# Group-norm chains, row norm, key landmarks and half the bias product rearranged in a two-stage attention kernel

## Chip, cores and metric

The kernel runs on one core of one Trainium2 chip. The metric is the device time of one execution in microseconds. TensorE does the matrix products, VectorE the reductions and elementwise work, ScalarE the activations and copies, GpSimd some elementwise work and the indirect DMAs, and SyncE issues most other DMAs. Each engine runs its own queue in order; semaphores join them.

## What is computed

16 images of 128 channels and 32x32 pixels (N = 1024) pass through six blocks, each added to its input: attention over pixels behind a group norm, convolutions behind a second group norm, landmark attention behind a row norm, a mixture of 8 experts with 2 chosen a row, a plain attention, and a mixture of 16 experts with 6 chosen. What the change touches, cut down:

```python
# block 1 and 2: norm over 8 groups (with weight and bias), then over 32 groups
xn = (xg - mean) * rsqrt(var + 1e-5);  xn = xn * norm_w + norm_b
# block 3: landmark attention, 8 heads of 16, 16 landmarks (every 64th row)
q, k, v = layernorm(t) @ Wqkv.T + bqkv
q_lm, k_lm = q[::64], k[::64]
kernel_1 = softmax(q @ k_lm.T * scale)
kernel_2 = softmax(q_lm @ k_lm.T * scale)
kernel_3 = softmax(q_lm @ k.T * scale)
z = kernel_2.T / sum(kernel_2 ** 2)
for _ in range(6): z = 2 * z - z @ kernel_2 @ z
t = t + (kernel_1 @ (z @ (kernel_3 @ v))) @ Wproj.T + bproj
# block 4: each row goes to its 2 best of 8 experts
scores = top2(softmax(layernorm(t) @ Wg))
t = t + sum_e scores[:, e] * (gelu(x @ W1[e] + b1[e]) @ W2[e] + b2[e])
```

## The kernel before

The program has four stages. **The first stage** (`attention_phase`) is the attention over pixels. Image by image, 64 slots (8 heads by 8 row tiles) go by; each holds a scores product that is read by a maximum on VectorE (L454), and a product with the shift (L693), an exponential on ScalarE (L597) and a product with the values (L706). Beside these, `plan` puts the next image's group norm into the first slots (`normed`: moments, the groups' sums, norm, the query, key and value products) and the previous image's projection and second group norm into slots 29 to 34 (`projected`). A ring of two PSUM banks (`ps_a`) is shared by the scores and these products: TensorE (PE) may write a bank only when VectorE or ScalarE has read what lay in it two uses before.

The group norm: the channels' moments (`channel_moments`, L75 to L80), a small product for the groups' sums (L655), then `group_affine` (L85 to L95): mean and mean of squares, variance, `rsqrt` by an integer guess and three Newton steps (L58 to L67), scale and shift. Each small VectorE operation is followed by a drain, so they make a chain. "norm" (L491 to L496) folds weight and bias in and writes the input `xn` of the query product (L663); "norm2" (L480 to L482) stores scale and shift in `gn2` for later and writes the normed second input, which "turn2" (L485) transposes.

**The convolutions** (`conv_phase`) follow and are untouched.

**The second stage** (`landmark_and_gelu_phase`) does the landmark attention and the 8 experts. `experts(i)` goes through 46 slots; in the even ones TensorE multiplies a 128-row tile by its expert's first weights (L1793), in the odd ones the tile before by the second weights (L1803), and ScalarE takes the gelu between them (L1609). Beside them run `front(i + 2)` (the landmark attention of the image two ahead), `choice(i + 1)` (row norm, router and row numbers of the next image) and `combine(i - 1)` (gathered results added, L1532). These are generators: `yield 17` means that what follows is placed behind the experts' own work of slot 17, in the queue of that engine. In one slot the order is experts, front, choice, combine. Ahead of the loop `front(0)` runs alone and `front(1)` beside `choice(0)`.

What the steps touch, by engine:

- Row norm of `choice`: `token_norm_steps` yields after each half of the statistics (n = 0, 1), after the variance (n = 2), after `rsqrt` (n = 3) and twice in the writes of the normed rows (L983). L1493 (`if n == 2: yield 4`) leaves the statistics and the variance in slot 0 and puts `rsqrt` and the writes in slot 4. TensorE turns the rows in slots 8 and 9 (L1738).
- In slot 4, ahead of that, `front` multiplies the convolutions' result in (L1336, L1338), behind the gate product (L1654, slot 2); TensorE turns the result in slot 6 (L1664).
- Landmarks: the query product (slot 15) and key product (slot 16) go to PSUM (L1654); ScalarE adds the biases (`qt` L1568, `kt` L1571); VectorE spreads the landmark columns over the heads (L1346, twice) in slot 17; TensorE multiplies all queries by the key landmarks in slot 18 (L1677) and all keys by the query landmarks in slot 19.
- Newton steps: slots 25 to 36, one product each that VectorE copies (L1398), and two that it takes from 2z (L1401, L1402). Beside the first step it sums `kernel_1`'s weights (L1406, L1408), beside the second it multiplies by the inverse (L1411). `k1_exp` says that ScalarE's exponentials of these weights are through.
- Bias product: scores times the experts' second bias, in two halves through one PSUM bank `pc` (L1768, slots 34 and 36); VectorE adds each half to the rows (L1518, slots 36 and 38) and then lets the bank go (`base_up`).
- Row numbers: VectorE's routing (L1441 on, slots 27 on) ends in `index_out` (L1465). GpSimd then scatters the normed rows to DRAM in expert order (L1313, 16 indirect DMAs), SyncE loads the first four tiles (L1238), TensorE turns them in the last slot (L1776) and ScalarE copies them (L1623).

**The dense stage** (`dense_attention_and_silu`) shares `token_norm_steps` and with it `rsqrt`.

## Time and profile before

| | us |
|---|---|
| median of 3 runs (5480.68 to 5505.98) | 5484.53 |
| the profiled execution | 5477.94 |
| its span, first to last instruction | 5476.1 |
| PE busy | 4820.5 (88%) |
| DVE busy | 3578.8 (65%) |
| ACT busy | 2948.8 (54%) |
| POOL busy | 1017.9 (19%) |
| mean granted clock of TensorE | 0.953 |

The engines are named PE (TensorE, matmul), PEld (its weight loads), DVE (VectorE), ACT (ScalarE), POOL (GpSimd) and SP (SyncE); a q behind a name means the engine's queue, as in SPq. All rows come from the profiled execution; times count from the start of its span. Busy time is no measure of the bound where stages differ, so the rows below go by stage. In a timeline the number in brackets is how long the engine stood idle before the instruction, and behind the arrow is what ended that. A granted clock of 1.00 is TensorE's upper level (2.4 GHz), 0.50 the lower (1.2 GHz).

### The profile page before, as it was taken

To read this page: it belongs to the slowest core of one execution; us is meant where nothing else is said; L and a number is where in the kernel's file an instruction comes from. 1 tells how busy PE (TensorE), PEld (TensorE's weight loads), DVE (VectorE), ACT (ScalarE), POOL (GpSimd) and SP (SyncE) were. 2 spreads that over 40 slices of the span, in tenths; PEclk is the share of its full clock that TensorE was granted. 3 is DMA by queue.
4 is the path that set the end of the run, shared out by engine and by line. 5 is a ranking of instruction groups with operands and counts; after the bars stand their busy time and mean duration, and the time that the engine had idled before them with its cause. 6 is when DMAs were issued, how large, how long until landed. Compare 5 with 4: busy or idle time off the path is not lost.

```text
span 5476.1 us, 81744 instructions
## 1 busy us (share of the span) xinstructions
PE 4820.5 (88%) x25601; PEld 2609.5 (48%) x25601; DVE 3578.8 (65%) x7699; ACT 2948.8 (54%) x5390; POOL 1017.9 (19%) x1348
## 2 busy tenths in 40 slices
PE   5888888888888886967999899999899999999999
PEld 1222222222222221335888888888755555555554
DVE  6677777777776772646666666665676766766765
ACT  2555566555655654423555555556655455555552
POOL 2211211121212212211434334343200000000000
PEclk7999999999999998987999999999999999999999
DMA  2522222222222221222555455554311111111112
GB/s 85 147 71 71 76 89 71 71 71 71 71 83 71 72 74 32 30 68 83 154 165 173 140 176 154 164 170 116 109 49 46 52 46 48 51 43 52 51 46 74
DMA packets 406296, 477.08 MB, mean 87 GB/s; under 512 B 87640, under 2 KB 249648, under 8 KB 403760
## 3 DMA queue, kind: packets, MB, share of 16 engines
q1 hardware_dynamic: 372128, 424.84, 25.5%
q0 software_dynamic: 20576, 35.55, 2.4%
q10 hardware_dynamic: 13168, 11.48, 0.8%
q8 instruction: 213, 3.49, 0.3%
q14 instruction: 211, 1.73, 0.1%
HBM read 308.54 MB, written 145.57 MB: 83 GB/s over the span
## 4 chain that ended last, share of the span: by engine, by line
PE 30%; DVE 12%; issue 4%; ACT 4%; DVEq 3%; POOL 2%; DMA 1%; ACTq 0%; SPq 0%; POOLq 0%
PE n_ps_f L2155 4%; PE n_ps_f L2148 4%; PE n_ps_xy L1803 3%; PE n_ps_h L1793 3%; PE n_ps_c L2195 2%; PE n_ps_h L2207 2%; POOL rows_scratch L1313 2%; PE n_ps_f L2142 2%; PE n_ps_f L1654 1%; PE n_ps_xy L2211 1%; PE n_ps_h L2211 1%; DVEq L2027 1%; DVE n_down_weights L2026 1%; PE n_ps_f L995 1%; ACT n_hidden L1609 1%
## 5 line engine op out<-in xcount | busy, mean ns | idle before, releaser
L597 ACT ACTIVATE a_probs<-ps_b 128x512 f32<-128x512 f32 x2048 | 1110.7, 594 | 800.4 <-PE ps_b L693 787.5
L454 DVE TENSOR_REDUCE a_negmax<-ps_a 128x1 f32<-128x1024 f32 x1024 | 1206.4, 1219 | 384.5 <-PE ps_a L637 374.8
L637 PE MATMUL ps_a<-a_k_stack,a_q_stack 96*128 96x512 bf16 x2048 | 635.6, 397 | 181.4 <-DVE a_negmax L454 89.8
L693 PE MATMUL ps_b<-a_q_stack,a_k_stack 99*128 99x512 bf16 x2048 | 675.0, 392 | 67.5 <-ACT a_probs L597 30.6
L1609 ACT ACTIVATE n_hidden<-n_ps_h,n_b 128x128 f32<-128x128 f32 x1472 | 420.4, 374 | 402.6 <-PE n_ps_h L1793 399.1
L706 PE MATMUL ps_o<-a_probs,a_v_ones 128*32 128x512 f32 x4096 | 561.8, 621 | 0.2 <-ACT a_probs L597 0.2
L637 PEld LDWEIGHTS ps_a<-a_k_stack,a_q_stack 96*128 96x128 bf16 x2048 | 146.3, 99 | 736.4 <-DVE a_negmax L454 470.2
L1803 PE MATMUL n_ps_xy<-n_down_weights,n_hidden 128*128 x2944 | 402.6, 280 | 56.1 <-ACT n_hidden L1609 30.2
L693 PEld LDWEIGHTS ps_b<-a_q_stack,a_k_stack 99*128 99x128 bf16 x2048 | 196.7, 100 | 486.4 <-ACT a_probs L597 247.0
L1803 PEld LDWEIGHTS n_ps_xy<-n_down_weights,n_hidden 128*128 128x128 f32 x2944 | 363.4, 193 | 86.7 <-issue 83.1
L2092 ACT ACTIVATE n_down_weights<-n_ps_h 128x512 f32<-128x512 f32 x288 | 172.4, 599 | 427.7 <-PE n_ps_h L2207 318.5
L1793 PE MATMUL n_ps_h<-n_xy,n_up_weights 128*128 128x128 f32 x2944 | 397.8, 279 | 3.1 <-DMA n_up_weights<-in_L_ffn_W_dram 1.7
L1313 POOL DMA_INDIRECT rows_scratch<-n_xln,n_index_out x256 | 256.9, 1004 | 719.2 <-DVE n_index_out L1465 642.3
L1793 PEld LDWEIGHTS n_ps_h<-n_xy,n_up_weights 128*128 128x128 f32 x2944 | 366.7, 194 | 26.1 <-issue 23.2
L1305 POOL DMA_INDIRECT n_rows<-outs_scratch,n_index_back x256 | 259.0, 1012 | 357.3 <-DMA outs_scratch<-n_xy 254.3
L410 POOL CAST a_shift<-a_shift 16x128 bf16<-16x128 f32 x192 | 54.0, 281 | 1315.1 <-DVEq L463 1297.7
L2155 PEld LDWEIGHTS n_ps_f<-n_xln,n_u_probs_t 128*128 128x128 f32 x2048 | 246.4, 192 | 59.8 <-issue 44.2
L2155 PE MATMUL n_ps_f<-n_xln,n_u_probs_t 128*128 128x128 f32 x2048 | 251.2, 276 | 1.6 <-ACT n_u_probs_t L2058 1.6
L2148 PE MATMUL n_ps_f<-n_qt 128*128 128x512 f32 x512 | 240.9, 593 | 0.0
L1977 DVE TENSOR_REDUCE e_negmax<-n_ps_f 128x1 f32<-128x1024 f32 x128 | 156.6, 1224 | 116.6 <-PE n_ps_f L2148 116.6
L2061 ACT ACTIVATE n_yt_probs<-n_ps_f,e_negmax 128x1024 f32<-128x1024 f32 x128 | 142.6, 1114 | 118.9 <-DVE e_negmax L1977 118.5
L2195 PE MATMUL n_ps_c<-n_down_weights,n_xt 128*128 128x512 f32 x384 | 198.8, 601 | 4.4 <-DVE n_down_weights L2033 4.4
(350 smaller groups left out, 7485.5 us busy)
## 6 DMA issues: line engine op xcount, KB each, us to landing
n_up_weights<-in_L_ffn_W_dram SPq DMA_DIRECT2D x368, 256.0 KB
n_up_weights<-score_scratch SPq DMA_DIRECT2D x512, 128.0 KB, 2.9
split_scratch<-a_pieces SPq DMA_DIRECT2D x180, 256.0 KB
a_q_stack<-split_scratch SPq DMA_DIRECT2D x128, 192.0 KB, 3.4
a_k_stack<-split_scratch SPq DMA_DIRECT2D x128, 192.0 KB, 4.0
rows_scratch<-n_zero SPq DMA_DIRECT2D x16, 1472.0 KB
outs_scratch<-n_xy SPq DMA_DIRECT2D x176, 128.0 KB
n_xg<-rows_scratch SPq DMA_DIRECT2D x80, 256.0 KB, 4.7
```

Source lines behind the costliest of these rows:

```text
L454: dve.tensor_reduce(negmax[:, b, t:t + 1], bank, axis=AX.X, op=ALU.max, negate=True).then_inc(ring_read, 1)
L597: act.activation(probs[:, m % PROBS, 512 * k:512 * k + 512], ps_b[:, k, :], ACT.Exp).then_inc(b_exp, 1)
L637: last = pe.matmul(bank[:, cols], q_stack[0:KS, h, 128 * t:128 * t + 128], k_stack[0:KS, h, cols], start=True, stop=True)
L693: pe.matmul(ps_b[:, k, :], k_stack[:, h, 128 * t:128 * t + 128], q_stack[:, h, 512 * k:512 * k + 512], start=True, stop=True).then_inc(b_u ...
L706: last = pe.matmul(ps_o[32 * j:32 * j + 32, 512 * k:512 * k + 512], v_ones[:, t, J * g + j, :], probs[:, (J * quad + j) % PROBS, 512 * k:5 ...
L1313: gp.indirect_dma_start(x_dram[i][:, :], bass.IndirectOffsetOnAxis(index_out[:, k, t:t + 1], 0), xln2[:, t, :], None).then_inc(scattered, 16)
L1609: last = act.activation(hidden[:, j % 2, f, :], ps_h[j % 2][:, 128 * f:128 * f + 128], ACT.Gelu, bias=b1[:, bass.ds(e, 1), f:f + 1].rearra ...
L1793: last = pe.matmul(ps_h[j % 2][:, 128 * f:128 * f + 128], up_weights[:, j % RING, 128 * f:128 * f + 128], rows_t, start=True, stop=True)
L1803: last = pe.matmul(ps_xy[:, col:col + 128], hidden[:, j % 2, f, :], own_down[:, f, :], start=(f == 0), stop=(f == FT - 1))
L2148: last = pe.matmul(pa[:, 512 * k:512 * k + 512], qt[:, 128 * t:128 * t + 128], qt[:, 512 * k:512 * k + 512], start=True, stop=True)
L2155: last = pe.matmul(pb[:, 0:C], probs_t[:, (t - 1) % 2, m, :], xln[:, m, :], start=(m == 0), stop=(m == NT - 1))
L2195: last = pe.matmul(ps_o[:, :], wd(unit), mixed[(i * STEPS + n) % 3], start=False, stop=(unit == UNITS - 1), skip_group_check=True)
```

## The change

`rsqrt` no longer makes a negative half of its input first: the factor goes into an operation that was there, so it has 10 operations for 11. A new `rsqrt_column` for one column takes minus half of the variance and needs 7. `group_affine` becomes `group_scale`: it forms minus half of the variance directly and leaves the shift to its callers. "norm" needs one operation for the shift where it had two, and "norm2" writes the scale straight into `gn2` and makes the shift there. In the second stage, the key landmarks are made from the key product in PSUM, with the bias added in the same operation; ScalarE's copy of the keys waits for them, and the product of all keys waits for that copy. The sum of `kernel_1`'s weights moves ahead of the first Newton step, its inverse stays where it was. The row norm's `rsqrt` goes to slot 0. The second half of the bias product goes from slot 36 to 39, VectorE's part of it from 38 to 40.

```diff
 def rsqrt(dve, y, v, t):
     dve.tensor_scalar(y.bitcast(I32), v.bitcast(I32), -0.5, 1597463007.0, ALU.mult, ALU.add)
-    dve.drain()
-    dve.tensor_scalar(v, v, -0.5, None, ALU.mult)
     for _ in range(3):
         dve.drain()
         dve.tensor_tensor(t, y, y, ALU.mult)
         dve.drain()
-        dve.tensor_tensor(t, t, v, ALU.mult)
+        dve.scalar_tensor_tensor(t, t, -0.5, v, ALU.mult, ALU.mult)
         dve.drain()
         last = dve.scalar_tensor_tensor(y, t, 1.5, y, ALU.add, ALU.mult)
...
+def rsqrt_column(dve, out, y, minus_half, t):
+
+    dve.tensor_scalar(y.bitcast(I32), minus_half.bitcast(I32), -0.5, 519526879.0, ALU.mult, ALU.add)
+    dve.drain()
+    for n in range(3):
+        dve.scalar_tensor_tensor(t, y, minus_half, y, ALU.mult, ALU.mult)
+        dve.drain()
+        dve.scalar_tensor_tensor(out if n == 2 else y, t, 1.5, y, ALU.add, ALU.mult)
+        dve.drain()
...
-def group_affine(dve, scale, shift, group, sums, sums_read, width, small, eps):
+def group_scale(dve, scale, group, sums, sums_read, width, small, eps):
     dve.tensor_scalar(group[:, :], sums, 1.0 / width, None, ALU.mult).then_inc(sums_read, 1)
     dve.drain()
-    dve.tensor_tensor(small[:, 0:1], group[:, 0:1], group[:, 0:1], ALU.mult)
+    dve.scalar_tensor_tensor(small[:, 0:1], group[:, 0:1], 0.5, group[:, 0:1], ALU.mult, ALU.mult)
     dve.drain()
-    dve.tensor_tensor(small[:, 1:2], group[:, 1:2], small[:, 0:1], ALU.subtract)
+    dve.scalar_tensor_tensor(small[:, 1:2], group[:, 1:2], -0.5, small[:, 0:1], ALU.mult, ALU.add)
     dve.drain()
-    dve.tensor_scalar(small[:, 1:2], small[:, 1:2], 0.0, eps, ALU.max, ALU.add)
+    dve.tensor_scalar(small[:, 1:2], small[:, 1:2], 0.0, -0.5 * eps, ALU.min, ALU.add)
     dve.drain()
-    rsqrt(dve, scale, small[:, 1:2], small[:, 2:3])
-    dve.scalar_tensor_tensor(shift, group[:, 0:1], -1.0, scale, ALU.mult, ALU.mult)
-    dve.drain()
+    rsqrt_column(dve, scale, small[:, 0:1], small[:, 1:2], small[:, 2:3])
...
                 elif what == "norm2":
-                    dve.tensor_copy(gn2[:, 0, bass.ds(prev, 1)], gscale[:, :])
-                    dve.tensor_copy(gn2[:, 1, bass.ds(prev, 1)], gshift[:, :])
-                    dve.tensor_scalar(xn[:, :], x1[:, :], gscale[:, :], gshift[:, :], ALU.mult, ALU.add)
+                    scale, shift = gn2[:, 0, prev:prev + 1], gn2[:, 1, prev:prev + 1]
+                    dve.scalar_tensor_tensor(shift, group[:, 0:1], -1.0, scale, ALU.mult, ALU.mult)
+                    dve.drain()
+                    dve.tensor_scalar(xn[:, :], x1[:, :], scale, shift, ALU.mult, ALU.add)
...
                     dve.tensor_tensor(gscale[:, :], gscale[:, :], nw[:, :], ALU.mult)
-                    dve.tensor_tensor(gshift[:, :], gshift[:, :], nw[:, :], ALU.mult)
                     dve.drain()
-                    dve.tensor_tensor(gshift[:, :], gshift[:, :], nb[:, :], ALU.add)
+                    dve.scalar_tensor_tensor(gshift[:, :], group[:, 0:1], gscale[:, :], nb[:, :], ALU.mult, ALU.subtract)
                     dve.drain()
-                    dve.tensor_scalar(xn[:, :], xf[:, :], gscale[:, :], gshift[:, :], ALU.mult, ALU.add).then_inc(xn_up, 1)
+                    dve.tensor_scalar(xn[:, :], xf[:, :], gscale[:, :], gshift[:, :], ALU.mult, ALU.subtract).then_inc(xn_up, 1)
...
-                for src, dst, up in ((qt, q_lm, 1), (kt, k_lm, 2)):
-                    dve.wait_ge(S["qk_up"], i * 2 + up)
-                    last = dve.tensor_tensor(dst[:, :].rearrange("p (h l) -> p h l", h=HEADS), b16,
-                                             src[:, 0:N:STEP].unsqueeze(1).broadcast_to((128, HEADS, LM)), ALU.mult)
-                last.then_inc(S["lm_up"], 1)
+                every = lambda ap: ap[:, 0:N:STEP].unsqueeze(1).broadcast_to((128, HEADS, LM))
+                by_head = lambda ap: ap[:, :].rearrange("p (h l) -> p h l", h=HEADS)
+                dve.wait_ge(S["qk_up"], i * 2 + 1)
+                dve.tensor_tensor(by_head(q_lm), b16, every(qt), ALU.mult)
+                dve.wait_ge(S["qk_ps"], i * 2 + 2)
+                dve.scalar_tensor_tensor(by_head(k_lm), every(pa), kb[:, :], b16, ALU.add, ALU.mult).then_inc(S["lm_up"], 1)
...
                 dve.tensor_scalar(zt[:, :], m2[:, :], fro[:, :], None, ALU.mult).then_inc(S["z0_up"], 1)
+                dve.wait_ge(S["k1_exp"], i + 1)
+                dve.tensor_reduce(sum1[:, :], k1v, axis=AX.X, op=ALU.add)
+                dve.drain()
...
                     if it == 0:
-                        dve.wait_ge(S["k1_exp"], i + 1)
-                        dve.tensor_reduce(sum1[:, :], k1v, axis=AX.X, op=ALU.add)
-                        dve.drain()
                         dve.reciprocal(sum1[:, :], sum1[:, :])
...
-                    if n == 2:
+                    if n == 3:
                         yield 4
...
-                    yield 36 + 2 * k
+                    yield 36 + 4 * k
                     dve.wait_ge(S["b2_ps"], i * HALVES + k + 1)
...
                 act.wait_ge(S["qk_ps"], i * 2 + 2)
+                act.wait_ge(S["lm_up"], i + 1)
                 act.activation(kt[:, :], pa[:, :], ACT.Identity, bias=kb[:, :]).then_inc(S["qk_up"], 1)
...
                 yield 19
+                pe.wait_ge(S["qk_up"], i * 2 + 2)
                 wide(pa, q_lm[:, :], kt).then_inc(S["s3_ps"], 1)
...
-                    yield 34 + 2 * k
+                    yield 34 + 5 * k
                     if k:
                         pe.wait_ge(S["base_up"], i * HALVES + 1)
```

## Rows read from the trace of the kernel before

**Rows 1.** Busy time by stretch: start:end, us, busy of each engine (instructions), PEclk, DMA, GB/s.
```profile
92.00:2082.00 1990.00, 1745.94 (x8524) 489.80 (x8524) 1416.24 (x1835) 1184.66 (x2105) 404.38 (x673) 0.96 0.25 79
2472.00:3840.00 1368.00, 1219.34 (x9231) 1100.34 (x9232) 836.05 (x2911) 757.85 (x1896) 476.56 (x480) 0.96 0.50 150
```

**Rows 2.** Waits of PE, 2472 to 3840 us: total us, times, longest.
```profile
PE n_ps_c L1738 <- DVE n_xln L983: 22.7, 16, 3.2
PE n_ps_c L1768 <- DVE maps L1518: 20.5, 16, 1.4
PE n_ps_xy L1803 <- ACT n_xy L1623: 17.8, 17, 1.3
PE n_ps_f L1702 <- DVE n_small L1398: 15.8, 32, 1.2
PE n_ps_f L1677 <- DVE n_small L1346: 11.3, 15, 1.6
```

**Rows 3.** PE in order of time, one image: start, us, line, tiles, xcount [idle before].
```profile
2989.35 1.04 PE L1664 MATMUL n_ps_f<-c_ident,n_u_probs_t 128*128 128x128 f32 x8
...
3035.42 0.49 PE L1702 MATMUL n_ps_f<-n_small 128*128 128x128 f32 x2 [0.67 <-DVE n_small L1398]
...
3063.89 0.44 PE L1776 MATMUL n_ps_xy<-c_ident,n_xg 128*128 128x128 f32 x2 [0.95 <-DMA n_xg<-rows_scratch]
```

**Rows 4.** DVE in order of time, the same image.
```profile
2985.76 1.28 DVE L1336 SCALAR_TENSOR_TENSOR n_u_probs_t<-n_ps_f,n_b,n_u_probs_t 128x1024 f32<-128x1024 f32 x1 [3.24 <-PE n_ps_f L1654]
...
2996.23 0.17 DVE L58 TENSOR_SCALAR n_inv<-n_var 128x8 int32<-128x8 int32 x1
...
2999.01 2.14 DVE L983 TENSOR_SCALAR n_xln<-n_tok_next,n_mv,n_inv 128x128 f32<-128x128 f32 x8
...
3010.73 0.38 DVE L1346 TENSOR_TENSOR n_small<-c_block,n_kt 128x128 f32<-128x128 f32 x1 [2.89 <-ACT n_kt L1571]
...
3026.72 0.29 DVE L1398 COPY n_small<-n_ps_f 128x128 f32<-128x128 f32 x1 [1.59 <-PE n_ps_f L1699]
...
3028.64 1.22 DVE L1406 TENSOR_REDUCE n_sum<-n_xln 128x64 f32<-128x1024 f32 x1
...
3037.05 0.17 DVE L1465 CAST n_index_out<-n_place 128x16 uint32<-128x16 f32 x1
```

**Rows 5.** Line L1336, all of it: idle time before, ended by: us, times.
```profile
  PE n_ps_f L1654: 27.0, 16
```

**Rows 6.** ACT in order of time, the same image.
```profile
3009.57 1.13 ACT L1571 ACTIVATE n_kt<-n_ps_f,n_kb 128x1024 f32<-128x1024 f32 x1
```

**Rows 7.** Busy time by stretch, 7 us behind the bias product, two images of 14.
```profile
3049.00:3056.00 7.00, 7.00 (x64) 6.88 (x63) 3.71 (x12) 1.77 (x6) 5.17 (x7) 1.00 0.31 101
3135.00:3142.00 7.00, 7.00 (x49) 6.88 (x48) 2.15 (x8) 0.85 (x2) 5.17 (x7) 0.76 0.33 111
```

**Rows 8.** POOL in order of time, first and last of 16 scatters.
```profile
3038.00 0.99 POOL L1313 DMA_INDIRECT rows_scratch<-n_xln,n_index_out  x1 [31.30 <-DVE n_index_out L1465]
...
3057.46 1.27 POOL L1313 DMA_INDIRECT rows_scratch<-n_xln,n_index_out  x1 [0.30 <-issue]
```

**Rows 9.** SP in order of time: the load of the scattered rows.
```profile
3060.99 0.38 SPq L1238 DMA_DIRECT2D n_xg<-rows_scratch  x1
```

**Rows 10.** DVE in order of time, first stage, two images.
```profile
1067.92 3.58 DVE L454 TENSOR_REDUCE a_negmax<-ps_a 128x1 f32<-128x1024 f32 x3 [2.05 <-PE ps_a L637]
...
1256.02 0.81 DVE L496 TENSOR_SCALAR a_xn<-a_xf,a_gscale,a_gshift 128x1024 f32<-128x1024 f32 x1
1256.96 2.36 DVE L454 TENSOR_REDUCE a_negmax<-ps_a 128x1 f32<-128x1024 f32 x2
```

**Rows 11.** Waits of PE, 92 to 2082 us.
```profile
PE ps_a L663 <- DVE a_negmax L454: 13.0, 12, 1.6
```

**Rows 12.** PE in order of time, first stage, one image.
```profile
1255.24 1.18 PE L637 MATMUL ps_a<-a_k_stack,a_q_stack 96*128 96x512 bf16 x4 [1.73 <-DMA a_k_stack<-split_scratch]
...
1258.24 3.78 PE L663 MATMUL ps_a<-a_xn,a_wqkv 128*128 128x512 f32 x4 [0.96 <-DVE a_negmax L454]
```

More of the change, by code:

```diff
@@ L477, in step @@
                     width, eps = ((C // 8, 1e-5), (C // 32, 1e-5))[work[1]]
-                    group_affine(dve, gscale[:, :], gshift[:, :], group, bank[:, 0:2], ring_read, width, small, eps)
+                    scale = gn2[:, 0, prev:prev + 1] if work[1] else gscale[:, :]
+                    group_scale(dve, scale, group, bank[:, 0:2], ring_read, width, small, eps)
                 elif what == "norm2":
-                    dve.tensor_copy(gn2[:, 0, bass.ds(prev, 1)], gscale[:, :])
-                    dve.tensor_copy(gn2[:, 1, bass.ds(prev, 1)], gshift[:, :])
-                    dve.tensor_scalar(xn[:, :], x1[:, :], gscale[:, :], gshift[:, :], ALU.mult, ALU.add)
+                    scale, shift = gn2[:, 0, prev:prev + 1], gn2[:, 1, prev:prev + 1]
+                    dve.scalar_tensor_tensor(shift, group[:, 0:1], -1.0, scale, ALU.mult, ALU.mult)
+                    dve.drain()
+                    dve.tensor_scalar(xn[:, :], x1[:, :], scale, shift, ALU.mult, ALU.add)
                     dve.drain()
```

## The prediction

> **What bounds the kernel now.** I read the views in this order: the busy time by stage, TensorE's waits inside the second stage, one image of that stage on each engine in order of time, and the same for one image of the first stage. The attention over pixels (first stage) takes the span's first 2.19 ms, the convolutions go on to 2.39 ms, the landmark attention with the experts (the second stage, to which five of the six edits belong) lasts until about 3.84 ms, and the dense attention takes the rest. In both stages that the change touches TensorE is the engine nearest to full: 88% of the first loop, 89% of the second; VectorE has 71% and 61% [rows 1]. Both stages are one order written by hand, so each engine is an in-order queue, and time is lost where TensorE stands at a wait. So a cut on VectorE is worth only what it takes from a wait of TensorE, and a wait removed is worth only what the next wait doesn't take back.
>
> In the second stage the waits repeat from image to image, with a period of 85.5 us: on average 1.4 us for the turn of the row norm's result (22.7 over 16), 1.3 for the second half of the bias product (20.5 over 16), 0.75 for the product with the key landmarks (11.3 over 15), and in the Newton steps two that make 0.25 and 0.67 in each of the loop's 14 images (with those ahead of the loop 15.8 over 32) [rows 2, 3]. These the change is aimed at. Two others matter for where the gain goes: the rows for the next image's experts come by DMA at the end of each image (0.95 of wait in the image shown), and behind them TensorE waits 1.05 for ScalarE's copy (17.8 over 17) [rows 2, 3].
>
> **The change, part by part.** I price against the profiled execution, 5477.94 us with a span of 5476.1; the median of the three runs, 5484.53, lies 6.6 us above it, and I take that distance over to the changed kernel.
>
> *Row norm.* The inverse root of the experts' row norm (11 small VectorE operations; 2.78 us, by the same sequence of the other norm [rows 4]; 10 now, some 2.53) moves from behind the u product (slot 4) to ahead of it (slot 0). Its result was 1.4 us late for TensorE; 2.78 us earlier it isn't late any more. What it moves ahead of is the product L1336, for which VectorE sits idle until TensorE's L1654 is through: 27.0 us over 16, on average 1.7, in the loop mostly 0.7 to 3.2 [rows 4, 5]. The root takes more than that in most images, so L1336 starts up to 1.8 us later. TensorE needs the result at L1664: from the start of L1336 (2985.76) it and L1338 take 2.59 us, to 2988.35, and L1664 starts at 2989.35 [rows 3, 4]. So 0.9 us of the delay are free, and up to 0.9 could show as a new wait. I take nothing for it, since the wait for rows at the end of the image gives VectorE a longer idle time there (below). Of the 22.7 us I take 20: in the image ahead of the loop nothing lies beside the chain, and most of the wait remains.
>
> *Key landmarks.* VectorE read the key landmarks from ScalarE's biased copy and waited 2.89 us for it [rows 4]; now it reads the product itself, complete some 2.2 us earlier. TensorE's wait is gone, 11.3 us, and about 1 more in the first image, ahead of that stretch. The new operation (PSUM operand, a bias column, 128x128) isn't in the trace; a copy of this size from PSUM takes 0.29, the operation replaced 0.38 [rows 4]; I take 0.38, and the difference hides in those 2.2 us at either end. The added wait stands in ScalarE's queue: its copy of the keys now follows VectorE's landmarks, and behind it are a copy of rows and an expert's activations. ScalarE began that copy at 3009.57, after other work [rows 6]; the landmarks would be ready near 3008.9, so the wait is met. The product with all keys, which gets a wait of its own, stands behind two more groups of TensorE's queue, some 3 us after the copy's end: nothing.
>
> On this the Trainium skill's PSUM — Partial Sum Buffer, section "PSUM bank collisions raise a hardware error", says that two engines mustn't read one bank at once, so the copy can't run beside the landmarks' read and the order costs what VectorE is late. By the rows it is early by 0.7 us, and the sum stays the same by either; the section only makes this cover the one to look at.
>
> *Key weights' sum.* The reduction (1.22 us [rows 4]) leaves the stretch between the first and the second Newton step for the place before the first. There VectorE is idle 1.59 us until TensorE's product comes [rows 4], so it fits with 0.3 to spare; the running sums behind it are needed 2.7 us after they were ready, 1.4 after the shift. From the first step on VectorE works without a break until the row numbers are out (3037.2 [rows 4]), about 0.8 us earlier now; not by the whole 1.22, as it then waits for the second step's product. TensorE's waits of 0.25, 0.16 (between the two, a product that waits for the first step's result) and 0.67 shrink to about 0.3 together: 0.78 in 14 images, 11 us.
>
> *Half the bias product later.* The wait of 1.3 is gone: TensorE multiplies the second half three slots later, when VectorE has long read the first. In 9 of the 14 images the granted clock is 0.76 over the 7 us behind that wait, so it stood at the lower of its two levels (1.2 of 2.4 GHz) for about half of them; in the other 5 it is 1.00 [rows 7]. From the row numbers to the turn of the new rows TensorE takes 27.0 us in the first kind, 25.5 in the second (worked out image by image, from pairs as in rows 3 and 4); without wait and fall it would be some 24.1. But the rows must arrive first: GpSimd starts its 16 scatters 0.78 us after the row numbers, ends the last 20.7 later, SyncE issues the load 2.3 after that (1.3 in most images), and it lands 2.9 on, where TensorE waits [rows 3, 4, 8, 9]. This chain takes 25.4 us at best and 26.3 on average over the 14 (two scatter slower, three loads land late). So of 26.74 us on average only about 0.45 can go: 6 us. The rest turns into a longer wait for rows, some 2 us an image, with the 1.05 behind it. The place of VectorE's half in its queue (behind the mixed copy, ahead of the combination's sums) costs nothing, as VectorE idles 3 us before the image's last product.
>
> *What that wait costs.* After a wait of 1.3 the clock fell in 9 images of 14; at the image's end (0 to 0.95 and 1.05) in 1 of 14. With 2 and 1.05 it should fall in most; I charge 1.5 us (27.0 less 25.5) in two images of three, 14 us. Bounds: none, and twice 1.5 in every image, 42 us.
>
> *First stage.* Each group norm loses 6 small operations in a chain, 0.24 us each [rows 4]: 1.4 us, two chains an image. The one after the projection hides: VectorE then idles 2.05 us (0.7 at least) for TensorE's scores [rows 10]. The one before the queries doesn't: the maxima start right behind the norm (at 1256.96, after 1256.02 and 0.81), and TensorE's L663 waits 0.96 for the first; 13.0 us in 12 images [rows 10 to 12]. The change can't win all of it, as the scores themselves come late: L637 starts at 1255.24, a maximum can begin 0.65 later, and L663 follows 1.28 after that, unless TensorE is busy until then [rows 10, 12]. That gives 0.3 to 1.1 an image, 8 us in all. The first norm of all and the last stand alone: 1.4 each, 3 us. Bounds of the stage: 3 and 16.
>
> *Dense attention.* Its norms also lose one operation, 0.25 us, beside other work: 1 us.
>
> **Sum:** 20 + 12 + 11 + 6 - 14 + 8 + 3 + 1 = 47, and some 2 us because the first matmuls after a wait are slower: 49 us. So 5478 - 49 = 5429 in a profiled execution, **5435** as a median.
>
> **Rivals.** *The row norm's new place is paid for.* If the end of the image doesn't lengthen VectorE's idle time, the root delays L1336 beyond its cover, L1664 waits up to 0.9, and the clock falls behind that. For: that idle time is below 1.5 us in ten images. Against: the wait for rows lies just ahead. Price: 0.9 and 1.5 in 14 images, 34 us, less a few: near 5465. *The chain of rows doesn't bind.* If VectorE reaches the row numbers earlier by the whole 1.22 of the reduction, or if the loads land in 25.4 us every time, most of the bias wait is won as well and no fall follows: 14 + 14 us or so more, 5407. Against: VectorE waits for TensorE's product in the second Newton step. *Slower:* the wait for rows and the wait for the copy together put TensorE on the lower clock for much longer at the beginning of each image. It decides from 4.4 us lost per image (47 + 14 us over 14), three times what one fall cost; at 6 us per image the time is 5484.5 - 63 + 84 = 5506. For: in the first stage, behind two waits so close, L663's four matmuls take 3.78 us [rows 12]. Against: work resumes in between. *The change doesn't do what it says:* if the landmarks' read still waits for work ahead of it on VectorE, 12 us fall out, 5447, inside the forecast's own range.
>
> **How the numbers follow.** Forecast 0.58, own range 5415 to 5453; the row norm's place 0.18; rows not binding 0.16; slower 0.05; a mixture 0.03. The measurement tells 0.5% from no change, 27 us, so faster means below 5457. The forecast and the chain that doesn't bind lie below it, and a part of the first rival: faster 0.77, same 0.18, slower 0.05. The range runs from the one rival to the other, 5404 to 5468.
>
> **What would show it.** Right: TensorE's waits at L1738, L1677 and L1768 gone; the wait for the rows' DMA near 2 us in every image, with GpSimd's first scatter still 0.8 us behind the row numbers; the granted clock at 1.00 behind the bias product and below it at the start of most images; L663's wait at a third. Wrong: a wait of TensorE for L1338's result; an image period above 84 us; waits for rows that sum to under 10 us.

## The result, and the profile after

| | before | after |
|---|---|---|
| median of the runs, us | 5491.98 (5480.68 to 5505.98) | 5415.56 (5415.53 to 5422.59) |
| the profiled execution | 5477.94 | 5415.53 |
| its span | 5476.1 | 5413.7 |
| last scores product of the first stage starts at | 2071.3 | 2041.3 |
| from the first to the last row numbers | 1288.1 | 1258.4 |

The ratio is 0.9863, with an interval of 0.9835 to 0.9890: 75 us faster, where 49 were forecast, and 5415.56 us where 5435 stood. Between the two profiled executions the difference is 62 us: 30 from the first stage, 30 from the second, nearly 3 from all else. The remaining 13 are not in the traces: the profiled execution of before was the quickest of its runs.

Busy time by stretch of the changed kernel, the counterpart of [rows 1] (start:end, us, busy of PE, PEld, DVE, ACT and POOL with instructions, granted clock, DMA share, GB/s); the stretches end 30 and 60 us earlier, with the same work in them:

```profile
92.00:2052.00 1960.00, 1730.12 (x8524) 485.33 (x8524) 1398.13 (x1660) 1184.75 (x2105) 404.27 (x673) 0.97 0.26 80
2442.00:3780.00 1338.00, 1215.09 (x9246) 1104.05 (x9247) 829.97 (x2879) 757.51 (x1896) 473.38 (x480) 0.95 0.52 154
```

In the first stage TensorE's instructions are as many as before, 8524, but their busy time fell by 15.8 us (1745.94 before): the same work at a higher clock (0.97 for 0.96 on average). In the second stage it stayed, 1215.09 against 1219.34, while the stretch became 30 us shorter: there the standing went.

TensorE's waits in the second stage (total us, times, longest), the counterpart of [rows 2]:

```profile
PE n_ps_xy L1787 <- DMA n_xg<-rows_scratch: 31.7, 15, 7.8
PE n_ps_xy L1814 <- ACT n_hidden L1619: 28.8, 14, 2.2
PE n_ps_xy L1814 <- ACT n_xy L1633: 17.2, 17, 1.3
PE n_ps_f L1713 <- DVE n_small L1410: 12.8, 19, 1.5
PE n_ps_c L1749 <- ACT n_xt L1600: 6.8, 16, 0.7
```

The wait for the new rows in the kernel before:

```profile
PE n_ps_xy L1776 <- DMA n_xg<-rows_scratch: 5.3, 6, 3.1
```

The waits for the normed rows, the bias product and the key landmarks are gone. The largest is now the one for the new rows: 31.7 us, 5.3 before, in every image of the loop. In the Newton steps 12.8 of 15.8 us are left, and a wait has come up in the place of the one for the normed rows: 0.4 us an image for ScalarE's copy of the turned rows.

One image of the changed kernel, TensorE in order of time (start, us, line, tiles; in brackets the idle time before), then GpSimd's first and last scatter with SyncE's load; the counterparts of [rows 3, 8, 9]:

```profile
2991.78 0.49 PE L1713 MATMUL n_ps_f<-n_small 128*128 128x128 f32 x2 [0.67 <-DVE n_small L1410]
...
3018.79 0.44 PE L1787 MATMUL n_ps_xy<-c_ident,n_xg 128*128 128x128 f32 x2 [1.05 <-DMA n_xg<-rows_scratch]
3020.30 1.15 PE L1814 MATMUL n_ps_xy<-n_down_weights,n_hidden 128*128 x8 [1.07 <-ACT n_xy L1633]
3021.46 2.03 PE L1804 MATMUL n_ps_h<-n_xy,n_up_weights 128*128 128x128 f32 x8
```

```profile
2994.37 0.99 POOL L1321 DMA_INDIRECT rows_scratch<-n_xln,n_index_out  x1 [30.01 <-DVE n_index_out L1474]
...
3013.76 0.96 POOL L1321 DMA_INDIRECT rows_scratch<-n_xln,n_index_out  x1 [0.30 <-DVEq L1533]
...
3016.00 0.38 SPq L1246 DMA_DIRECT2D n_xg<-rows_scratch  x1
```

From the row numbers (out at 2993.6) to the turn TensorE takes 25.2 us here and 25.86 on average over the 14 images (25.2 to 27.9), of which it stands 1.7. Without that it would be 24.15; "some 24.1" was forecast. Behind the two waits eight products take 2.03 us that otherwise take 1.06: the clock. The 7 us behind the beginning of three images (first, second and fourth line), and the 7 us around a later wait of the second of them (third line; 70 us behind the row numbers, for `n_hidden`). The last number but two is the granted clock:

```profile
2850.00:2857.00 7.00, 5.04 (x22) 4.64 (x23) 4.25 (x28) 0.97 (x3) 0.00 (x0) 0.56 0.82 231
3021.00:3028.00 7.00, 6.99 (x37) 5.88 (x36) 4.84 (x28) 2.77 (x9) 0.37 (x1) 0.76 0.59 174
3064.00:3071.00 7.00, 6.59 (x44) 6.60 (x45) 2.53 (x8) 2.76 (x9) 0.00 (x0) 0.76 0.32 98
3104.00:3111.00 7.00, 6.75 (x44) 5.40 (x45) 5.96 (x30) 2.67 (x9) 0.00 (x0) 1.00 0.67 196
```

Taken over all 14 images, the clock is below 1.00 behind the bias product in none (9 before), at the image's beginning in 8 (1 before), around the 14 waits for `n_hidden` in 11 (5 before). By the granted clock in the two traces TensorE is on its lower level for 72 us of the loop (second to last row numbers), 48 before.

### The profile page after: what moved, and what is told of

Read it like the earlier page. It is cut to its first block and busy times, and to the rows that moved or that the text cites. A ratio compares the mean times of both kernels' runs of the same rounds, so it can differ in the third digit from the quotient of the medians.

```text
span 5413.7 us, 81296 instructions
## 1 busy us (share of the span) xinstructions
PE 4801.5 (89%) x25601; PEld 2611.1 (48%) x25601; DVE 3547.7 (66%) x7443; ACT 2948.8 (54%) x5390; POOL 1014.3 (19%) x1348
## 5 line engine op out<-in xcount | busy, mean ns | idle before, releaser
L1804 PE MATMUL n_ps_h<-n_xy,n_up_weights 128*128 128x128 f32 x2944 | 415.3, 287 | 2.2 <-issue 1.4
L1814 PEld LDWEIGHTS n_ps_xy<-n_down_weights,n_hidden 128*128 128x128 f32 x2944 | 364.1, 193 | 85.4 <-issue 83.7
L1804 PEld LDWEIGHTS n_ps_h<-n_xy,n_up_weights 128*128 128x128 f32 x2944 | 382.7, 202 | 26.3 <-issue 22.0
```

Of the source, the lines that this page charges most:

```text
L1804: last = pe.matmul(ps_h[j % 2][:, 128 * f:128 * f + 128], up_weights[:, j % RING, 128 * f:128 * f + 128], rows_t, start=True, stop=True)
L1814: last = pe.matmul(ps_xy[:, col:col + 128], hidden[:, j % 2, f, :], own_down[:, f, :], start=(f == 0), stop=(f == FT - 1))
```

## Experiments

Times are medians of the runs, ratios stand to the kernel before on the same chips. "Rows" is the time from the first to the last row numbers in the profiled execution, 16 images; the before kernel's own second stage gave 1288.1, 1305.2, 1291.4 and 1290.9 in the four kernels that left it as it was, so differences in this column below some 15 us say little for kernels built on before. The medians were not all taken on one chip, and so the small differences depend on the measure: by the ratios the four edits taken back cost 0, 7, 4 and 18 us against the changed kernel (bias product, row norm, weights' sum, key landmarks), by the medians 7, 11, 10 and 20, and by this column 7, 14, 11 and 17. Of the four only the landmarks' runs all lie above the changed kernel's; the sizes of the others are rough.

| kernel | median us | ratio, interval | rows us |
|---|---|---|---|
| changed | 5415.56 | 0.9863 (0.9835 to 0.9890) | 1258.4 |
| before, both norm chains short | 5458.25 | 0.9931 (0.9916 to 0.9946) | 1305.2 |
| before, norm before the queries short | 5469.27 | 0.9959 (0.9942 to 0.9975) | 1291.4 |
| before, norm after the projection short | 5498.68 | 1.0006 (0.9997 to 1.0016) | 1290.9 |
| changed, bias product back | 5422.30 | 0.9862 (0.9844 to 0.9879) | 1265.1 |
| before, bias product later | 5492.82 | 0.9994 (0.9983 to 1.0005) | 1293.0 |
| changed, row norm back | 5426.55 | 0.9875 (0.9858 to 0.9893) | 1272.6 |
| changed, weights' sum back | 5425.41 | 0.9870 (0.9853 to 0.9887) | 1269.1 |
| changed, key landmarks back | 5435.51 | 0.9895 (0.9874 to 0.9915) | 1275.1 |
| changed, weights normalised ahead | 5394.60 | 0.9818 (0.9799 to 0.9837) | 1244.7 |
| the same, row numbers earlier | 5391.40 | 0.9814 (0.9800 to 0.9828) | 1233.4 |
| the same, bias product back | 5402.24 | 0.9830 (0.9817 to 0.9844) | 1245.8 |

### The first stage: which norm, and is it waits alone?

Before, with `group_scale`, `rsqrt_column` and the short endings of "norm" and "norm2" from the change's diff, and nothing of the second stage:

> The kernel before with the first stage's shorter norm chains alone. Theory (waits and the clock): the first stage ends some 30 us earlier, as in the changed kernel (last scores product near 2042 us, 2072 before): about 11 us are waits of TensorE, the query product's wait for the maxima falling from 13.0 to about 6, and the rest is clock, because that wait is what the query products' lower clock follows. The time falls by 28 to 32 us. Rival (waits alone): the norms are worth the waits that they shorten, 8 + 3 us, and the other 19 us of the first stage come from something else; the time falls by about 11.

The same for "norm" alone, "norm2" on the old chain:

```diff
-    group_affine(dve, gscale[:, :], gshift[:, :], group, bank[:, 0:2], ring_read, width, small, eps)
+    if work[1]:
+        group_affine(dve, gscale[:, :], gshift[:, :], group, bank[:, 0:2], ring_read, width, small, eps)
+    else:
+        group_scale(dve, gscale[:, :], group, bank[:, 0:2], ring_read, width, small, eps)
```

> The kernel before with the shorter chain in the norm before the queries alone; the norm after the projection keeps the long chain. Theory: the query products' wait and the clock behind it belong to this norm, about 1.7 of the 2.1 us an image: 22 to 26 us faster than before. Rival (both norms share it, because the alternation of the clock's falls couples the two places of an image): 10 to 18 us faster.

And for "norm2" alone, the two branches the other way round:

> The kernel before with the shorter chain in the norm after the projection alone. Theory: this norm is hidden but for 0.1 to 0.4 us an image and the last image; the first stage's last scores product ends within 6 us of the kernel before (2072), the time falls by 0 to 8 us. Rival (the two norms share the gain): the first stage ends 10 to 18 us earlier.

The scores products of the first stage in both norms short, "norm" alone and "norm2" alone (times; shortest, median, longest in ns; first and last start in us), and the query products' wait in the last two:

```profile
L647 PE MATMUL ps_a<-a_k_stack,a_q_stack x2048: 376/379/634, 51.9 to 2043.4; 96*128 96x512 bf16 x187
...
L663 PE MATMUL ps_a<-a_k_stack,a_q_stack x2048: 376/379/634, 52.2 to 2042.5; 96*128 96x512 bf16 x187
...
L665 PE MATMUL ps_a<-a_k_stack,a_q_stack x2048: 376/379/634, 52.5 to 2074.3; 96*128 96x512 bf16 x187
```

```profile
PE ps_a L689 <- DVE a_negmax L478: 6.3, 13, 0.7
...
PE ps_a L691 <- DVE a_negmax L478: 11.8, 12, 1.5
```

The first two end where the changed kernel does, the third where before does. So the stage's 30 us are the norm before the queries, all of them, and the norm after the projection is hidden, as the prediction had it. The medians agree: 38 us (30 to 46) for both, 22.5 (14 to 32) for "norm" alone, nothing for "norm2"; the 11 between the first two have no counterpart in their first stages, which end within 1 us of each other, and stay open. The 30 us themselves are good to some 7: in the kernel before with the bias product later, whose first stage is that of before, the last scores product starts at 2078.1. The size is the point. The wait itself gave 7.3 us (13.0 [rows 11], now 5.7). Most of the rest is clock. First the query products of before, then of the changed kernel (line, count | busy us, mean ns | idle before), then those of two images of the changed kernel, the counterpart of [rows 12], and of one image of before that didn't wait:

```profile
L663 PE MATMUL ps_a<-a_xn,a_wqkv 128*128 128x512 f32 x120 | 83.9, 837 | 13.0 <-DVE a_negmax L454 13.0
```

```profile
L671 PE MATMUL ps_a<-a_xn,a_wqkv 128*128 128x512 f32 x120 | 75.4, 762 | 5.7 <-DVE a_negmax L461 5.7
...
481.74 3.59 PE L671 MATMUL ps_a<-a_xn,a_wqkv 128*128 128x512 f32 x4 [0.45 <-DVE a_negmax L461]
...
859.92 1.98 PE L671 MATMUL ps_a<-a_xn,a_wqkv 128*128 128x512 f32 x4 [0.45 <-DVE a_negmax L461]
```

```profile
1129.56 3.62 PE L663 MATMUL ps_a<-a_xn,a_wqkv 128*128 128x512 f32 x4
```

Four query products behind a wait of 0.96 took 3.78 us in [rows 12]. In the changed kernel, mostly behind 0.45, they take 1.98 in four of 15 images, 2.34 in one and 3.25 to 3.78 in ten (1.98 in a single one with both norms short); before, they took 2.88 in one and 3.37 to 3.78 in the others, two of them without a wait. So the shorter wait doesn't end the fall of the clock behind it. What changed is how long TensorE stays on the lower level: by the granted clock in the traces 150 us of the stage before (31 stretches), 113 in the changed kernel (26) and with both norms short (30), 106 with "norm" alone (27), 154 with "norm2" alone (30). The 120 query products lost 8.5 us of busy time and the stage's other products the rest of the 15.8. With 13 us of waits (7.3 here, 5.0 for the loads of `a_k_stack`, 50.4 before and 45.4 now, 0.8 for maxima) that is the stage's gain. That the clock's part comes with "norm" is shown; why the stretches got shorter isn't.

### Half the bias product: taken back, and done alone

```diff
-                    yield 36 + 4 * k
+                    yield 36 + 2 * k
...
-                    yield 34 + 5 * k
+                    yield 34 + 2 * k
```

> The changed kernel with the second half of the bias product back in slot 36 and VectorE's part in 38. Theory (the chain of row numbers, scatters and load binds): from the row numbers to the landing of the rows it still takes about 25 us, the wait of 1.35 us comes back behind the bias product, and the wait for rows shrinks by as much; the time stays within 8 us of the changed kernel's. Rival (the edit is worth the wait that it removed): 14 waits of 1.35 us and more come back and nothing goes, 19 us slower than the changed kernel, 30 with the clock behind them.

The reverse of this diff on the kernel before:

> The kernel before with half the bias product later, alone. Theory (the chain of rows binds): TensorE's wait of 1.35 us goes, the wait for rows grows from 0.2 to about 1.3 us an image; from the row numbers to the turn 26.7 us become about 25.7, 14 us faster at most, and 5 less for the clock at the image's beginning: 5 to 14 us faster than before. Rival (nothing binds behind it): 14 x 1.35 and 9 falls of the clock go, 19 + 14, 30 us faster.

TensorE's waits in the second stage, first with the product back, then in before with the product later:

```profile
PE n_ps_c L1779 <- DVE maps L1527: 20.7, 16, 1.4
...
PE n_ps_xy L1787 <- DMA n_xg<-rows_scratch: 13.3, 7, 3.3
```

```profile
PE n_ps_xy L1776 <- DMA n_xg<-rows_scratch: 33.6, 15, 9.5
```

Taken back, 20.7 us of wait return and 18.4 of the wait for rows go (31.7 to 13.3), and the kernel is 7 us slower, less than the runs of either differ. Done alone, 20.5 us of wait go [rows 2] and 28.3 come, and the time is the same: 0.9994, where 5 to 14 us were expected. The clock is why even the 0.9 us an image that TensorE gains up to the turn (25.86 for 26.74) are not seen: by the granted clock TensorE is on the lower level for 72 us of the loop, 48 before. Two of the 14 images of before with the product later, the 7 us at their beginning:

```profile
2648.00:2655.00 7.00, 7.00 (x37) 5.77 (x37) 3.27 (x18) 2.77 (x9) 0.33 (x1) 0.76 0.58 184
2734.00:2741.00 7.00, 7.00 (x40) 6.04 (x40) 3.30 (x18) 2.66 (x9) 0.00 (x0) 0.78 0.53 167
```

In all 14 the clock is below 1.00 here, from 0.52 to 0.78, and in none behind the bias product. The fall moved with the standing.

### Row norm, weights' sum and key landmarks, each taken back

```diff
-                    if n == 3:
+                    if n == 2:
                         yield 4
```

> The changed kernel with the row norm's root back in slot 4. Theory: TensorE's wait of about 1.15 us for the normed rows comes back in each of 14 images and the 0.4 us that it now waits there for ScalarE's copy goes, 0.75 net, and in both kernels the product behind the convolutions doesn't wait: 10 to 17 us slower than the changed kernel. Rival (the wait for rows gives it back): the later images arrive later at the wait for rows and wait less there; under 5 us slower.

For the sum, its three lines (`wait_ge` on `k1_exp`, `tensor_reduce`, `drain`) go back under `if it == 0:`.

> The changed kernel with the sum of the weights back between the first and the second Newton step. Theory (by the trace after): the wait of 0.67 us in the third Newton step stands in both, only the two short ones before it (0.25 and 0.16) come back, and the row numbers come later by up to that: 3 to 8 us slower. Rival (the forecast): three waits come back, 0.78 an image and the clock with them, 11 to 16 us slower.

For the landmarks, the loop over `qt` and `kt` and both queues without the added waits:

> The changed kernel with the key landmarks made from ScalarE's copy again. Theory: 0.69 us of wait comes back in each of 14 images and about 2.4 ahead of the loop, 10 to 14 us slower than the changed kernel. Rival (given back at the wait for rows): the images arrive later at the rows, under 4 us slower.

The waits that return, in this order:

```profile
PE n_ps_c L1749 <- DVE n_xln L991: 17.6, 15, 3.5
...
PE n_ps_f L1713 <- DVE n_small L1407: 15.1, 29, 1.2
...
PE n_ps_f L1685 <- DVE n_small L1354: 11.3, 15, 1.6
```

By the medians the row norm is worth 11 us, at the theory's lower end: 17.6 us return and 5.7 of the 6.8 of ScalarE's copy go. The weights' sum is worth 10, between the two expectations: TensorE stands only 3 us more in the loop, and the clock is below 1.00 at the beginning of 12 images for 8; the time and the standing don't agree, and how the rest divides stays open. The landmarks are worth 20, above either: 12 in the loop and 6 in the two images ahead of it (the time from the stage's first product to the second row numbers is 209.2 us for 203.2), where 2.4 were expected. None of the three is given back at the wait for rows (32.1, 30.1 and 34.4 us): they come ahead of the row numbers, and so they move the start of the chain along with them. The three and the bias product add up to 48 us by the medians and to 28 by the ratios; 37 are left of the 75 after the first stage's 38.

### What starts the chain: the row numbers earlier

If the chain from the row numbers to the landing binds, an earlier start must pay. The inverse and the product that follow the sum go ahead too:

```diff
                 dve.tensor_reduce(sum1[:, :], k1v, axis=AX.X, op=ALU.add)
                 dve.drain()
+                dve.reciprocal(sum1[:, :], sum1[:, :])
+                dve.drain()
...
                     dve.tensor_copy(mz[:, :], pa[:, 0:128]).then_inc(mz_up, 1)
+                    if it == 0:
+                        dve.tensor_tensor(k1v, k1v, sum1..., ALU.mult).then_inc(S["k1_up"], 1)
...
-                    if it == 0:
-                        dve.reciprocal(sum1[:, :], sum1[:, :])
-                        dve.drain()
-                    if it == 1:
-                        dve.tensor_tensor(k1v, k1v, sum1..., ALU.mult).then_inc(S["k1_up"], 1)
```

> The changed kernel, and the inverse of the weights' sum moves ahead of VectorE's first Newton copy, the product with it (1.23 us) between that copy and the first update, where VectorE stands idle for 1.3 us. Theory (the chain of row numbers, scatters and load binds): the row numbers come about 1.3 us earlier against TensorE's work, the wait for rows falls from 1.7 to about 0.5 an image, the 0.67 of the third Newton step goes, and most of the clock's falls at the image's beginning go: period 83.7 to about 82.2, 18 to 28 us faster than the changed kernel. Rival (the chain doesn't bind, TensorE's own work does): only the 0.67 can go, and part of it turns up elsewhere; 0 to 9 us faster.

21 us faster than the changed kernel, as the theory had it, but not by its way: the Newton wait of 0.67 is gone, and the wait for rows is what it was, 32.6 us. VectorE in one image shows why (the last two steps of the routing, and the Newton update in between):

```profile
2983.60 0.21 DVE L1469 TENSOR_REDUCE n_place<-n_high 128x8 f32<-128x64 f32 x1
2984.07 0.29 DVE L1417 SCALAR_TENSOR_TENSOR n_small<-n_small,n_ps_f 128x128 f32<-128x128 f32 x1 [0.26 <-PE n_ps_f L1713]
...
2984.95 0.17 DVE L1473 CAST n_index_out<-n_place 128x16 uint32<-128x16 f32 x1
```

The place of each row was known at 2983.8, but the row numbers stand in the next slot, behind an update for which VectorE waits for TensorE. So their place against TensorE's work can't change, however early VectorE is: the period fell from 83.7 to 82.6 us, by the 0.67 and what follows it, not by the chain. Hence the next kernel, with the counts a slot earlier on both engines, and the row numbers ahead of that update:

```diff
-                yield 27
+                yield 26
                 dve.wait_ge(S["count_ps"], i + 1)
...
-                    if n % 2:
-                        yield 27 + n // 2
+                    if n % 2 and n != 3:
+                        yield {1: 27, 5: 28, 7: 29}.get(n, 27 + n // 2)
...
-                yield 26
+                yield 25
                 pe.wait_ge(S["score_up"], i + 1)
```

> The kernel with the weights' normalisation ahead, and now the count product a slot earlier (25 for 26) and VectorE's routing with it, so that the row numbers come in slot 29, ahead of an update for which VectorE waits for TensorE. Theory (the chain from the row numbers to the landing binds, and the row numbers hung on their slot, which is why the last kernel shortened the period but left the wait for rows at 1.7 us an image): the row numbers come about 1.5 us earlier against TensorE's work, the wait for rows falls from 23.8 us over 14 images to 5 to 10, most falls of the clock behind it go; period 82.6 to about 81.2, 12 to 28 us faster than with the weights ahead alone, near 5375. Rival (VectorE's Newton copies now come late for TensorE, because the routing is packed denser between them): the wait moves to the Newton products, within 6 us of the kernel with the weights ahead.

Its row numbers in the same image, now ahead of the update, and its wait for rows in the whole stage:

```profile
2979.50 0.17 DVE L1473 CAST n_index_out<-n_place 128x16 uint32<-128x16 f32 x1
...
2980.23 0.29 DVE L1417 SCALAR_TENSOR_TENSOR n_small<-n_small,n_ps_f 128x128 f32<-128x128 f32 x1 [0.48 <-PE n_ps_f L1713]
```

```profile
PE n_ps_xy L1786 <- DMA n_xg<-rows_scratch: 11.1, 5, 6.4
```

The wait for rows is gone but in the image ahead of the loop and in four others, and the rows' time is 11 us shorter. In the medians only 3 us of it are seen, with runs from 5386 to 5404 and from 5386 to 5398: so the earlier rows and the shorter wait are shown, the 12 to 28 us that were expected of them are not. Part of the gain is taken by a wait that the changed kernel doesn't have in its loop, TensorE's for the product behind L1346 (2.6 us in six images). And the bias product once more, in this kernel:

> The kernel with the earlier row numbers, and the second half of the bias product back in slot 36 and VectorE's part in 38. Theory (the edit's worth hangs on what binds behind it): with the rows early the wait of 1.35 us is no longer covered, so putting it back costs 14 x 1.35 = 19 us, less what wait for rows is left, with the clock falls behind it: 12 to 30 us slower than the kernel with the earlier rows. Rival (the edit is worth nothing wherever it stands): within 6 us of it.

```profile
PE n_ps_c L1778 <- DVE maps L1526: 20.7, 16, 1.4
...
PE n_ps_f L1673 <- DVE n_u_probs_t L1346: 10.8, 12, 4.7
...
PE n_ps_xy L1786 <- DMA n_xg<-rows_scratch: 3.4, 5, 2.0
```

The same 20.7 us as above return, but now only 7.7 go, and the time is 10.8 us longer (rows 12.4). In the loop the same edit takes 10 us of standing off TensorE where the chain of rows binds (98 to 88) and 19 where it doesn't (87 to 68). In the time 0 to 7 of it are seen in the one case and 11 in the other; the times alone wouldn't tell 7 from 11. It is a little less than the 12 to 30 that were expected: by the granted clock TensorE is on the lower level for 38 us of this loop, 55 with the product later. The kernel with the earlier row numbers, 5391.4 us, has the lowest median of all: 1.9% below before, 24 us below the changed kernel.

## Why the prediction was right, and where it was off

**What bounds.** Right: in-order queues in which only a wait of TensorE counts. Every edit that moved the time moved one of the waits named.

**Row norm**, 20 forecast: 11 by the medians, 7 to 14 by the other measures. The new place cost nothing: in the loop of the changed kernel L1674, the product behind L1346, doesn't wait. The prediction's reason holds too: where the wait for rows is shorter, L1674 does wait, 3.3 us in six images with the bias product back, 6.1 in eleven with it back and the rows early (L1673 above). The term was too large because removing the wait uncovered the next one, ScalarE's copy of the turned rows, 0.4 us an image; the sum had no term for what stands behind the wait.

**Key landmarks**, 12 forecast: 20 (12 of it in the loop). The cover held: ScalarE, in the same image as [rows 6],

```profile
2965.04 0.35 DVE L1357 SCALAR_TENSOR_TENSOR n_small<-n_ps_f,n_kb,c_block 128x128 f32<-128x128 f32 x1 [0.61 <-PE n_ps_f L1664]
...
2966.10 1.13 ACT L1581 ACTIVATE n_kt<-n_ps_f,n_kb 128x1024 f32<-128x1024 f32 x1
```

begins its copy 0.7 us after the landmarks are made, without a wait, the very margin that was worked out. The new operation takes 0.35 (0.38 taken). On the Trainium skill's PSUM — Partial Sum Buffer, section "PSUM bank collisions raise a hardware error": the order that it asks for between two readers of one bank cost nothing in any of the loop's 14 images, and 2.28 and 1.57 us of waiting on ScalarE in the two images ahead of it.

**Weights' sum**, 11 forecast: 10 by the medians, 4 by the ratios. Near in size, wrong in its way. The forecast had 0.25, 0.16 and 0.67 shrink to 0.3; the first two went, the 0.67 of the third step stayed in every image, since it hangs on the product of 1.23 us with the inverse, which the change left in place. Taking that away too gave 21 us.

**Bias product and the clock at the image's beginning**, 6 - 14 = -8 forecast: a gain of 0 to 7 by the kernel that puts it back, none by the one that does it alone. The chain binds as it was laid out; it took 25.86 us, between the "best" and the "average" of the prediction. The fall of the clock came in 8 images of 14, and where two of three were charged; it costs some 1.15 us (periods of 84.0 us in four images with the fall, against 82.8 in six without it, the wait for rows being 1.3 and 1.4 on average; all ten have the later fall at `n_hidden`, and the one image with the first fall alone and an ordinary scatter has 82.3), not 1.5. What the sum didn't have is the third place: around the wait for `n_hidden`, unchanged at 2.1 us, the clock now falls in 11 images where it fell in 5.

**First stage**, 8 + 3 forecast: 30. This is the step that failed: 19 us too small, more than the whole difference between 49 and 62, and the second stage, where 35 stood and 30 came, gave 5 of it back. The wait was sized right (8; 7.3 measured, though 5.7 of 13.0 is not the third that was to be left). The sum put the clock in this stage at nothing, and the bounds of "3 and 16" were built from waits alone; half the stage's gain is clock, 15.8 us of busy time. The prediction had read the 3.78 us of the query products off [rows 12] and used them as an argument for the slower rival. That they show a low clock was in the trace: the next four query products of the same images take 1.98. But asking what they take without the wait wouldn't have given the size either, since most of them are still slow behind the shorter wait.

**Restarts and median.** The 2 us for slow first matmuls have no row of their own, and no run tests them. The 6.6 us between execution and median were carried over to the changed kernel; there the distance is nil, since its runs lie within 0.13% of each other. So 5415.56 stands at the very edge of the range of 5415 to 5453, and that it lies inside owes something to luck: a first stage that was 19 us better than forecast was in part made up for by a second that was worse.

**Rivals.** The row norm's place was not paid for. By the time alone the rival without a binding chain would have been nearer (5407, against 5435); the trace decides against it, as TensorE waits for the rows in every image of the loop, 1.05 us at least. And the clock didn't stay low long enough at the image's beginning for the slower case (4.4 us an image would have been needed, some 1.15 were lost in an ordinary one). The period of 83.7 us (13 periods, without the last image's) lies just under the 84 that the prediction set.

## To carry to other kernels

A wait of TensorE can have two prices, its own length and the clock: compare the products behind the wait with the same products elsewhere in the trace. Where they differ, leave room for the clock in the bounds, but don't take the whole difference as what a shorter wait brings. A wait that stands inside a chain with its own length (row numbers, scatters, load) is worth nothing to the end of that chain; what pays is an earlier start, and the start is set by the slot it stands in, not by when its data are ready. What moves the start along with it (here three of the four edits of the second stage) keeps its gain.

## What the runs showed of the hardware

The clock's falls are not tied to one wait. In the changed kernel the images in the rows above have nearly the same two waits at their beginning (1.05 and 1.07; 1.11 and 1.07), and the one has the clock at 0.76 behind them, the other at 1.00. Taking out one wait made it fall at others that had been there before without a fall, and in the last experiment, with more standing than in the kernel it is built on (86.5 us in the loop for 67.9), the clock was below 1.00 in fewer stretches (8 for 13). What decides between them isn't shown here.

On the Trainium skill's TensorE: Matmul & The Clock Gate, section "HAM oscillation — how this bites in real kernels", which tells of a kernel whose clock falls at each wait for a load of its loop, waits of some 3 to 5 us where those here are 1.0 to 3.8: the 14 of 14 image beginnings of before with the product later agree with it, the 8 of 14 of the changed kernel agree only in part.

In the changed kernel GpSimd's 16 scatters take 20.3 us in most images and 22.8 in two, the fifth and the twelfth of the stage; in the kernel before the same two take 22.4, the others 20.0 to 20.9. Most of the difference, 1.9 us, is one gap behind the first scatter, with nothing in the trace that ends it:

```profile
2823.72 0.99 POOL L1321 DMA_INDIRECT rows_scratch<-n_xln,n_index_out  x1 [29.72 <-DVE n_index_out L1474]
2826.92 0.98 POOL L1321 DMA_INDIRECT rows_scratch<-n_xln,n_index_out  x1 [2.20 <-issue]
```

In the changed kernel TensorE's wait for rows is 3.8 us in these two, 1.05 to 2.0 in the others. Its cause wasn't tried.
